# Six buffers instead of four for h and gated h, and other steps for the projections, the sums and the split of B in a four-layer selective scan

## The reference, cut to what matters

```python
x_dbl = einsum('bkdl,kcd->bkcl', xs, x_proj_w)          # dts, B (16 rows), C (16 rows)
delta = softplus(einsum('bkrl,kdr->bkdl', dts, dt_proj_w) + bias)
def step(h, inp):                                        # along the sequence
    u_t, d_t, b_t, c_t = inp
    h = exp(d_t[..., None] * A) * h + (d_t * u_t)[..., None] * b_t[:, :, None, :]
    y = einsum('bkdn,bkn->bkd', h, c_t)                  # sum over 16 states
    return h, y
```

## Time and profile before

| | |
|---|---|
| median of three runs | 39801.25 us (39799.93 to 39808.25) |
| the profiled execution | 39791.34 us, its span 39789.5 us |
| mean granted TensorE clock | 0.885 of full |
| VectorE busy | 35015.5 us, 88% |
| GpSimd busy | 33757.8 us, 85% |
| TensorE busy | 32412.7 us, 81% |
| ScalarE busy | 18602.6 us, 47% |
| one body (96 steps), typical | 321 us; 104 of them |

### The profile page before, as it was taken

The page is one execution under the profiler, slowest core; times in us unless marked ns, Lnnn a source line. Parts: engine busy times, 40 slices in busy tenths (PEclk is TensorE's granted clock), DMA queues, the critical chain, the costliest instruction groups (busy, mean ns, idle before and its releaser), DMA issues. The chain is left out here.

```text
span 39789.5 us, 352570 instructions
## 1 busy us (share of the span) xinstructions
PE 32412.7 (81%) x74336; PEld 12680.4 (32%) x74336; DVE 35015.5 (88%) x19200; ACT 18602.6 (47%) x27581; POOL 33757.8 (85%) x14276
## 2 busy tenths in 40 slices
PE   3888888888874888888888874888888888876887
PEld 1333333333321333333333321333333333322334
DVE  6999999999967999999999967999999999965994
ACT  3555555555522555555555522555555555533552
POOL 1999999999962999999999962999999999963994
PEclk6999999999976999999999976999999999977996
DMA  4777777777764777777777764777777777775776
GB/s 143 232 231 231 233 231 232 232 231 231 233 229 158 232 232 232 231 234 232 232 232 232 232 233 152 233 232 231 232 232 233 231 232 233 231 239 178 232 232 199
DMA packets 2745420, 8903.33 MB, mean 224 GB/s; under 512 B 436233, under 2 KB 580113, under 8 KB 2731665
## 3 DMA queue, kind: packets, MB, share of 16 engines
q1 hardware_dynamic: 2743056, 8883.57, 72.4%
HBM read 8117.72 MB, written 764.47 MB: 223 GB/s over the span
## 5 line engine op out<-in xcount | busy, mean ns | idle before, releaser
L1019 POOL TENSOR_TENSOR gh<-h,csb 128x1024 f32<-128x1024 f32 x9984 | 23366.0, 2359 | 1624.5 <-DVE h L825 1452.4
L737 PE MATMUL psy<-gh,t_ident 128*128 128x512 f32 x39968 | 20118.9, 633 | 6.0 <-POOL gh L1019 6.0
L825 DVE TENSOR_TENSOR_SCAN h<-decay,state,slot 128x1024 f32<-128x1024 f32 x6864 | 16099.6, 2346 | 851.6 <-ACT state L968 26.0
L737 PEld LDWEIGHTS psy<-gh,t_ident 128*128 128x128 f32 x39968 | 7907.8, 202 | 9571.7 <-issue 8274.6
L803 DVE TENSOR_TENSOR slot<-du,slot 128x1024 f32<-128x1024 f32 x6864 | 8295.7, 1209 | 792.8 <-PE slot L674 792.7
L674 PE MATMUL slot<-bc,pick 96*128 96x512 bf16 x13744 | 4431.3, 406 | 4584.0 <-DVE h L825 4560.3
L875 ACT ACTIVATE decay<-delta,na 128x1024 f32<-128x1024 f32 x6872 | 7872.0, 1146 | 12.1 <-issue 9.9
L821 DVE TENSOR_TENSOR_SCAN h<-slot,state,bb 128x1024 f32<-128x1024 f32 x3120 | 7263.0, 2328 | 290.5 <-ACT state L884 288.1
L1036 POOL TENSOR_TENSOR bb<-du,bb 128x1024 f32<-128x1024 f32 x3124 | 7361.2, 2356 | 0.6
L875 ACT ACTIVATE slot<-delta,na 128x1024 f32<-128x1024 f32 x3120 | 3487.9, 1118 | 7021.0 <-DVE h L825 7021.0
L884 ACT COPY state<-h 128x1 f32<-128x1 f32 x9984 | 1845.8, 185 | 5254.3 <-DVE h L825 4159.0
(11 more groups left out here) (103 smaller groups left out, 16846.9 us busy)
## 6 DMA issues: line engine op xcount, KB each, us to landing
csb<-bcdram SPq DMA_DIRECT2D x6692, 512.0 KB, 4.3
csb<-bcdram SPq DMA_DIRECT2D x6656, 256.0 KB, 4.9
bb<-bcdram SPq DMA_DIRECT2D x2096, 512.0 KB, 5.3
bb<-bcdram SPq DMA_DIRECT2D x2080, 256.0 KB, 5.4
u<-useq SPq DMA_DIRECT2D x212, 1536.0 KB, 8.0
yseq<-ybuf SPq DMA_DIRECT2D x624, 512.0 KB, 6.1
ya<-yseq SPq DMA_DIRECT2D x420, 512.0 KB, 4.3
yb<-yseq SPq DMA_DIRECT2D x360, 512.0 KB, 5.1
```

The lines of the kernel that those rows point to most:

```text
L737: mm = pe.matmul(psy[:, cols], T["ident"][:, :], gh[s % RING][:, cols], start=(n == 0), stop=(n == NS - 1), skip_group_check=True)
L825: dve.tensor_tensor_scan(h[s % RING][:, order], decay[s % DECAY_RING][:, order], slot[s % 2][:, order], first, ALU.mult, ALU.add)\
L1019: pool.tensor_tensor(gh[s % RING][:], h[s % RING][:], csb[s % C_RING][:], ALU.mult)\
```

## The change

RING goes from 4 to 6, so that h and gh have six buffers each. In TensorE's and ScalarE's programs, and for the correction in VectorE's, work stands at other steps. No instruction is added or removed but for what more buffers need (two more buffers of gh are zeroed at the start of each scan stage).

```diff
-RING, DECAY_RING, C_RING, B_RING = 4, 3, 4, 3
+RING, DECAY_RING, C_RING, B_RING = 6, 3, 4, 3
-DELTA_AT = (1, 2)
-PARTS_AT, EXP_AT, LOG_AT, CORRECTION_AT, TAKE_AT, DU_AT = 3, 4, 5, 6, 11, 12
-SUM_AT = (6, 6, 7, 8, 9, 9)
+DELTA_AT = (0, 3)
+PARTS_AT, EXP_AT, LOG_AT, CORRECTION_AT, TAKE_AT, DU_AT = 4, 5, 6, 7, 11, 12
+SUM_AT = (7, 8, 9, 9, 9, 10)
-XDBL_AT = [(0, 12), (0, 12), (0, 13), (0, 14), (0, 15), (1, 0)]
+XDBL_AT = [(0, 12), (0, 12), (0, 13), (0, 14), (0, 15), (0, 15)]
-HI_AT, REST_AT, MID_AT, LESS_MID_AT, LO_AT = (1, 9), (1, 12), (1, 13), (1, 14), (2, 0)
+HI_AT, REST_AT, MID_AT, LESS_MID_AT, LO_AT = (1, 9), (1, 12), (1, 13), (1, 14), (1, 15)
```

## The result

The changed kernel takes **39887.2 us** (median of 16 runs, 39858.1 to 39908.8) where the kernel before takes 39802.8 (16 runs beside them): ratio 1.0021, 95% interval 1.0013 to 1.0028. It is 84 us slower; the forecast was 39645, faster.

The account below looks back on a forecast made before the run. VectorE, busy for 88% of the span, was taken as the bound. A gain of 9.1 less new waits of 7.6 gave 1.5 us a body, x 104 = 156 us: 39645 us, 0.4% faster, 8 in 10 range 39150 to 40020.

Parts of the forecast that it names:

- part 4: SUM_AT and CORRECTION_AT moves: idle at step 6, clock falls behind it, new waits of 7.6 us a body (0 to 13.2).
- part 3: DELTA_AT and PARTS_AT moves at the tile's start: VectorE's waits at states 4 and 5 go, gaining 9.1 us a body.
- The turn of the loop: VectorE's wait where the loop turns: 1.28 us a body, said to stay.
- Part 1: Ring of h, four to six buffers: the scan never waits for a gate, so 0, and no place for a loss.
- part 8: Zeroing two more buffers twice per stage: under 15 us in all, hidden by the first loads, so 0.
- The bound and the pairs: VectorE sets the pace; its paired waits at states 4 and 5, 1.42 and 0.59 us in tile 0, go.
- The idle time at the start of a tile: TensorE's idle before the fill of state 3 shrinks by a half projection's 1.04 us, from 3.06 to about 2.0.
- The idle time at step 6: TensorE's idle before the fill of state 9 grows from 2.10 to about 3.8 us in every tile.
- The second rival: The stall moves to state 12 and grows, long falls in all tiles: 426 us slower, 40225 us; chance 0.25.
- The first rival: The clock stays up more than forecast: 39190 us with three short falls a body, 38855 with none; chance 0.20.
- the third: Half of the waits at states 4 and 5 stay beside the new ones: 322 us slower, 40120 us; chance 0.07.
- The signs: No idle before states 4 and 5, 1 to 2.2 us before state 12, GpSimd busier, its reduction wait gone.

Follow-up runs that it names:

- e2: The changed kernel with RING back at 4, all new steps kept: 39841.3 us, ratio 1.0010 to the kernel before.
- e1: The kernel before with RING 6 alone, every step where it stood: 39844.3 us, ratio 1.0011 to the kernel before.
- e3: The changed kernel with twelve small matmuls on zeros behind the reduction of step 6: 38896.2 us, ratio 0.9772 to the kernel before.
- e6: The changed kernel with SUM_AT (7, 8, 9, 9, 10, 10), one more half sum behind the fill of state 12: 39421.5 us, ratio 0.9905.
- e5: The kernel before, RING 4, with two more memsets on VectorE in front of each scan stage's loop: 39834.8 us, ratio 1.0009.
- e7: The kernel before with the changed DELTA_AT, PARTS_AT, EXP_AT, XDBL_AT and LO_AT; RING, SUM_AT and CORRECTION_AT as before: 39299.4 us, ratio 0.9872.
- e10: The changed kernel with eight small matmuls on zeros behind the reduction of step 6: 39212.1 us, ratio 0.9847 to the kernel before.
- e4: The kernel before with eight small matmuls on zeros behind the reduction of step 0: 39112.8 us, ratio 0.9827.

## Why the prediction was wrong, point by point

The profiled execution of the changed kernel took 39891 us where the sum gave 39635: 256 us more. Four terms, idle times of VectorE added up over the run, come to 253. Such sums meet the span within some 20 us only (the work outside the loops, 17 us longer, is not in them), so a part of the close fit is chance.

- **The step that failed is the count in part 4**, "one without, three short, two long: 7.6 us". Measured over the 104 bodies, of six tiles 0.3 had no fall, 2.4 a short one and 3.3 a long one, and the waits at states 10 and 12 were 883.6 / 104 = 8.5 us a body. That is 0.9 above the forecast, **93 us**. The prices were a little high (1.07 and 2.2 forecast, 0.88 and 1.96 measured), the count more than made up for it. The rows had a warning: one body was read, where the fall behind 2.1 us of idle came once in six tiles. Over the run it came in 221 of 624, and behind the idle time before the fill of state 3, where this was 2.9 us or more, in all 415, long in 385. The "up to 3.4" for a long fall stands on no row; the long fall in tile 5 lengthened the path by 13.28 - 10.33 = 2.95.
- **The size of part 3 failed too.** It took 9.1 us a body for the pairs from the run's total, which holds 67 us of VectorE's idle time at the start of the four scan stages. The body that was read has 8.2 in its pairs (1.42 + 1.34 + 1.55 + 1.55 and four times 0.59), and over the run the change took away 863 us, 8.3 a body: **84 us** less than forecast.
- **The turn of the loop was taken as fixed at 1.28 us.** Over 100 turns it went from 1.24 to 1.84 in the mean, **60 us** (2.03 in the body shown). It comes with the new steps (e2) and not with the rings (e1). It is gone in e3, where the clock stays up, and in e6, where the path is shorter; what makes it longer stays open.
- **Part 1 was right about the rings as buffers, wrong in its words "a loss has no place".** Two more buffers brought two more memsets a stage, part 8 costed these at nothing, and by e5 they bring most of RING 6's 42 us; **16 us** of it are the new waits at state 1. Their cost is not their own time (7.3 us in e5).
- **The bound and the pairs: right in kind.** VectorE sets the pace. The pairs at states 4 and 5 are gone; e7 shows that the moves of DELTA_AT and PARTS_AT, with XDBL_AT and LO_AT beside them, do it without the rings and without SUM_AT.
- **The idle time at the start of a tile: right by luck.** The row of 2.07 us in the earlier trace rows is one half projection and not two (a half is two matmul records, as in the reduction). The other half stands behind the fill of state 4: `19905.33 1.12 PE L692 MATMUL psc<-dts,wdt 32*128 32x512 f32 x2`. So a half takes 2.00 us at 1.2 GHz, and 1.05 with the clock at 1.00, as in the changed kernel (19934.01 to 19935.06). The 1.04 was half of a misread row and met this 1.05. About 2.0 us of idle were forecast and 1.92 found in tiles 2, 3 and 5; tiles 1 and 4 have none left, and tile 0 has 4.2.
- **The idle time at step 6: right.** 3.8 us forecast, 4.06 found; the path grew by the 0.86 us that were worked out (10.33 in e3), within the slack.
- **The second rival** had the direction, and I gave it 0.25. Its own terms did not come: it was to decide above a mean wait of 1.52 us a tile, and the mean was 883.6 / 624 = 1.42, between the forecast's 1.27 and that. At 1.42 the kernel is slower all the same, because the pairs gave back less than 9.1 and the turn took more. Its 40225 us would have needed a long fall in every tile.
- **The first rival** (the clock stays up) is what e3 makes by hand: 38896. In the third, 4.5 + 7.6 - 9.1 is 3.0 and not 3.1, which moves nothing.
- **The signs.** GpSimd's wait for the reduction went from 112.1 us over the run to 6.2, as forecast; either half of the change does it alone (7.6 in e1, 1.2 in e2), and it gains nothing. GpSimd's busy share stayed at 85% instead of rising.
- By the Trainium skill, "TensorE: Matmul & The Clock Gate", section "Why this matters for your kernels", idle above about 3 us is to be left out. The 4.06 us and their price agree, and the prediction gave that rule too little weight: where TensorE was idle for 3.8 us or more, in tiles 1 to 5, the clock fell in all 520. The prediction read the rule as if shorter idle were free, which e10 contradicts: at 2.3 us, 316 us over e3.

## What to carry to other kernels

Work that fills an engine's idle time isn't free to move: before moving it, look for how long TensorE would then be idle and at the granted clock behind idle times of that length, over the whole run and not in one body, and price the path behind it at 1.2 GHz in every tile where it may fall. Take what a loop can save from its own turns, without the start of the stage. Where TensorE must wait between bursts and stands on a path without slack, matmuls on zeros in the gap can pay: here they gave back 991 us. Split a change into its parts on the chip even where the total moved by 0.2%: it held a gain of about 500 us (e7), a loss of a little more, and some 40 us that came with two memsets.

## What the runs showed of the hardware

- The clock's fall has no bound at 3 us of idle here: the share of tiles with a fall went down with the idle time. Idle of 4.06, 3.20, 2.34 and 1.47 us at one place of each tile was followed by a fall of the clock in 589, 456, 246 and 0 of 624 tiles, and gave 39887, 39627, 39212 and 38896 us. Each fall cost VectorE about 0.9 to 1.0 us (short) or 2.0 to 2.3 (long) there.
- The length of the last idle time alone does not decide. In the kernel before, with 2.10 us before the fill of state 9, the clock fell in 97 of 104 bodies in tile 1 and in one in tile 5. In e4 it fell behind 1.44 us or less in 132 of 312 tiles.
- Two more memsets in front of each scan stage's loop, 7.3 us of work over the run, came with 33 us, 15.7 of them as 31 waits of 0.5 us at one instruction in the 10 ms of layer 1. A difference of 0.1% between variants of such a kernel can be no more than that.
